# The last batch of an attention loop gets an order of its own: its two routers and a layernorm change places

## The reference

```python
x = _layernorm(x + _L0_attn_ref(x, Wq, Wk, Wv, Wo))      # 16 heads in 4 groups, head size 16
...
def _L0_attn_ref(x, Wq, Wk, Wv, Wo):
    ...
    scores = jnp.einsum('bqgrd,bkgd->bgrqk', q, k) * scale + bias     # causal, sqrt-distance bias
    attn = jax.nn.softmax(scores, axis=-1)
    o = jnp.einsum('bgrqk,bkgd->bqgrd', attn, v).reshape(B, S, Hd)
    return o @ Wo.T
...
# router: sigmoid scores over 32 experts, 4 of 8 groups of experts kept, 6 experts per token
w, idx = _gate(xf, gate_w)
c = jnp.zeros((T, E), xf.dtype).at[jnp.arange(T)[:, None], idx].add(w)
y = jnp.einsum('tei,te,edi->td', jax.nn.silu(g) * u, c, w22)          # g, u: xf by w11, w33 of each expert
shared = jax.nn.silu(xf @ sw1.T) * (xf @ sw3.T) @ sw2.T
...
x = _layernorm(x + y + shared)
```

## Time and profile before

| | |
|---|---|
| median of 3 runs | 549.81 us (547.13 to 551.17) |
| the profiled execution, its own time | 553.8 us |
| its span, first to last instruction | 552.0 us |
| mean granted clock of PE | 0.942 of full speed |
| busy PE, DVE, ACT, POOL | 467.1, 366.9, 321.2, 227.0 us |
| attention loop, body of batch 7 on DVE | 222.6 to 243.3 us of the span |
| stretch between the loops | 243.3 to 296.4 us |
| expert loop and the end | 296.4 to 552.0 us |

### The profile page before, as it was taken

The page is one execution under the profiler, slowest core; times in us unless marked ns, Lnnn a source line. Parts: engine busy times, 40 slices in busy tenths (PEclk is TensorE's granted clock), DMA queues, the critical chain, the costliest instruction groups (busy, mean ns, idle before and its releaser), DMA issues.

```text
span 552.0 us, 12954 instructions
## 1 busy us (share of the span) xinstructions
PE 467.1 (85%) x3218; PEld 387.1 (70%) x3219; DVE 366.9 (66%) x1711; ACT 321.2 (58%) x1087; POOL 227.0 (41%) x244
## 2 busy tenths in 40 slices
PE   4376778777988887879895999999999999999993
PEld 3254557665857565654354999999999999998772
DVE  4036477839596969887733776777777777771574
ACT  1069798848787888954102565555555555553024
POOL 0000000260616262747770656666666666664000
PEclk9769999869788879999997999999999999999998
DMA  4669659997768672339994555555555555521994
GB/s 134 147 227 263 145 138 269 248 258 191 195 156 209 165 197 60 132 107 409 417 415 123 161 166 157 154 157 164 152 159 150 171 162 164 156 73 59 420 416 172
DMA packets 67995, 107.91 MB, mean 196 GB/s; under 512 B 9189, under 2 KB 55018, under 8 KB 66416
## 3 DMA queue, kind: packets, MB, share of 16 engines
q1 hardware_dynamic: 53472, 74.62, 47.2%
q0 software_dynamic: 10752, 26.13, 14.3%
q10 hardware_dynamic: 3728, 6.65, 3.3%
HBM read 64.03 MB, written 43.33 MB: 195 GB/s over the span
## 4 chain that ended last, share of the span: by engine, by line
PE 45%; DMA 20%; DVE 9%; SPq 8%; POOL 6%; ACT 6%; issue 5%; POOLq 0%; ACTq 0%; DVEq 0%
PE bank L726 21%; PE bank L735 11%; POOL routed L1433 6%; DMA expert_w<-expert_out 6%; DMA k_scratch<-k_lo 5%; PE bank L716 5%; DMA k_pack<-k_scratch 4%; DVE s_neg L1012 4%; ACT probs L831 4%; SPq L431 3%; PE bank L500 3%; DMA xt<-xT 2%; SPq L382 1%; ACT pT L842 1%; SPq L396 1%
## 5 line engine op out<-in xcount | busy, mean ns | idle before, releaser
L1433 POOL DMA_INDIRECT routed<-rows,position x96 | 93.5, 974 | 193.3 <-DVE position L1176 164.9
L1443 POOL DMA_INDIRECT expert_out<-rows,out_row x128 | 130.8, 1022 | 84.7 <-issue 61.2
L831 ACT ACTIVATE probs<-s_neg,m_neg 128x128 f32<-128x128 f32 (+1 forms) x256 | 114.1, 450 | 43.6 <-DVE m_neg L1012 43.4
L1012 DVE CUSTOM_DVE_ANT_0 s_neg<-bank,bias_sb 128x128 f32<-128x128 f32 (+1 forms) x256 | 79.6, 352 | 59.6 <-PE bank L532 58.5
L930 ACT ACTIVATE eg<-bank 128x128 f32<-128x128 f32 x128 | 35.5, 278 | 83.5 <-PE bank L726 82.8
L735 PE MATMUL bank<-expert_w,ea 128*128 x256 | 78.4, 388 | 2.4 <-issue 0.9
L726 PEld LDWEIGHTS bank<-x1T,xn 128*128 128x128 f32 x512 | 67.8, 194 | 3.6 <-issue 0.3
L532 PE MATMUL bank<-k_pack,q_pack 128*128 128x256 f32 (+1 forms) x128 | 58.7, 467 | 13.5 <-DMA k_pack<-k_scratch 11.2
L726 PE MATMUL bank<-x1T,xn 128*128 128x128 f32 x512 | 68.5, 277 | 0.0
L937 ACT ACTIVATE rows<-bank,pick 128x256 f32<-128x256 f32 x128 | 60.1, 470 | 2.7 <-DVE out_row L1342 2.2
L920 ACT ACTIVATE x1T<-bank 128x256 f32<-128x256 f32 x128 | 49.3, 385 | 12.6 <-PE bank L716 12.6
(11 more groups left out here) (162 smaller groups left out, 807.0 us busy)
## 6 DMA issues: line engine op xcount, KB each, us to landing
xg_all<-routed SPq DMA_DIRECT2D x128, 137.5 KB, 2.2
expert_w<-expert_out SPq DMA_DIRECT2D x16, 768.0 KB, 13.0
expert_w<-expert_weights SPq DMA_DIRECT2D x9, 1024.0 KB, 17.8
q_pack<-q_scratch SPq DMA_DIRECT2D x32, 256.0 KB, 4.7
routed<-empty SPq DMA_DIRECT2D x8, 550.0 KB, 13.3
k_pack<-k_scratch SPq DMA_DIRECT2D x16, 256.0 KB, 6.9
expert_w<-expert_weights ACTq DMA_DIRECT2D x3, 1024.0 KB
xt<-xT SPq DMA_DIRECT2D x9, 256.0 KB, 7.1
```

The lines of the kernel that those rows point to most:

```text
L831: act.activation(probs[g % 2][qb][:, 2 * pair + r, :], s_neg[u][:, r, 0:n], ACT.Exp, bias=m_neg[:, u, r:r + 1], scale=-1.0, accum_out=row_ ...
L1012: dve.tensor_tensor_reduce(out=s_neg[u][:, r, 0:n], in0=SCORES[u][:, n * r:n * r + n], in1=bias_sb[:, REP * g + 2 * pair + r, SEQ - n:SEQ] ...
L1433: pool.indirect_dma_start(routed, bass.IndirectOffsetOnAxis(ap=position[b % ROW_BUFS][:, t, j:j + 1], axis=0), rows[b % ROW_BUFS][:, t, :] ...
L1443: pool.indirect_dma_start(expert_out, bass.IndirectOffsetOnAxis(ap=out_row[:, k:k + 1], axis=0), ey[k], None, bounds_check=TOKENS * TOPK - ...
```

## The change

Only the body of batch 7 (`ahead` is false) and what follows it are reordered; the instructions stay the same.

- The router of batch 5 is finished in groups 0 and 1 (`LAST_AT_UNIT`: piece 11 at unit (1, 3) in place of (3, 2)).
- Batch 6's layernorm moves up in the body: `project_out` to (1, 1), `ln_stats` to (1, 2), `ln_moments` and the root to (1, 3), `ln_apply` to (2, 0), `turn_x1` to (2, 1), `copy_x1t` to (2, 2), `gate` to (2, 3), that is ahead of `values(7, 0)` on PE; `gate_exps(6)` to the start of group 3.
- The router of batch 6 stands in group 3 on DVE (`LAST_NEXT_AT_UNIT`), all of it ahead of `invert(7, par, 1)`; its `ranks` stands at the end of PE's body, ahead of `values(7, 1)`.
- Behind the loop, batch 6's router is gone; `turn_x1(7)` stands between the two `shared_up(0, m)`, and ACT's `copy_x1t(7)` between the two `shared_silu(0, m)`.

```diff
# PE, body
-                        if g == 3 and u == 0 and two_behind:
+                        if (g, u) == ((3, 0) if ahead else (1, 2)) and two_behind:
                             ranks(b - 2, par)
-                        if g == 3 and u == 1 and one_behind:
+                        if (g, u) == ((3, 1) if ahead else (2, 1)) and one_behind:
                             turn_x1(b - 1, o)
+                        if (g, u) == (1, 1) and not ahead:
+                            project_out(b - 1, o)
+                        if (g, u) == (2, 3) and not ahead:
+                            gate(b - 1, o)
                     if g == 2:
                         values(b, par, 0)
...
+                if not ahead:
+                    ranks(b - 1, o)
# PE, behind the loop
             shared_up(0, 0)
+            turn_x1(last_b, 1)
             shared_up(0, 1)
-            ranks(last_b - 1, 0)
-            turn_x1(last_b, 1)
             gate(last_b, 1)
# ACT, body
+                    if g == 3 and not ahead:
+                        gate_exps(b - 1)
...
-                        if g == 2 and u == 2 and one_behind:
+                        if (g, u) == ((2, 2) if ahead else (1, 3)) and one_behind:
                             ln_first_root(b - 1)
-                        if g == 3 and u == 1 and one_behind:
+                        if (g, u) == ((3, 1) if ahead else (2, 2)) and one_behind:
                             copy_x1t(b - 1, o, h - 1 + par)
# ACT, behind the loop
-            gate_exps(last_b - 1)
             ln_first_root(last_b)
             shared_silu(0, 0)
+            copy_x1t(last_b, 1, last_b // 2)
             shared_silu(0, 1)
-            copy_x1t(last_b, 1, last_b // 2)
# DVE, body
+            LAST_AT_UNIT = {(0, 1): (0, 1), (0, 2): (2, 3), (0, 3): (4, 5), (1, 0): (6, 7), (1, 1): (8, 9), (1, 3): (10, 11)}
+            LAST_NEXT_AT_UNIT = {(3, 1): (0, 1, 2, 3, 4, 5), (3, 2): (6, 7, 8, 9), (3, 3): (10, 11)}
...
-                        if (g, u) == (2, 1) and one_behind:
+                        if (g, u) == ((2, 1) if ahead else (1, 2)) and one_behind:
                             ln_stats(b - 1, o, h - 1 + par)
-                        if (g, u) == (2, 2) and one_behind:
+                        if (g, u) == ((2, 2) if ahead else (1, 3)) and one_behind:
                             ln_moments(b - 1)
-                        if (g, u) == (2, 3) and one_behind:
+                        if (g, u) == ((2, 3) if ahead else (2, 0)) and one_behind:
                             ln_apply(b - 1, o, h - 1 + par)
                         if two_behind:
-                            for piece in AT_UNIT.get((g, u), ()):
+                            for piece in (AT_UNIT if ahead else LAST_AT_UNIT).get((g, u), ()):
                                 router_piece(b - 2, par, piece)
+                        if not ahead:
+                            for piece in LAST_NEXT_AT_UNIT.get((g, u), ()):
+                                router_piece(b - 1, o, piece)
# DVE, behind the loop
-            router_piece(b - 1, 0, 0)
             norm(b, 1, 1)
-            for piece in range(1, 6):
-                router_piece(b - 1, 0, piece)
             ln_stats(b, 1, b // 2)
             ln_moments(b)
-            for piece in range(6, 10):
-                router_piece(b - 1, 0, piece)
             ln_apply(b, 1, b // 2)
-            for piece in (10, 11):
-                router_piece(b - 1, 0, piece)
```

More of the change, by code:

```diff
@@ L632, in body @@
                         values(b - 1, o, 1)
-                    if g == 1 and one_behind:
+                    if g == 1 and one_behind and ahead:
                         project_out(b - 1, o)
-                    if g == 3 and one_behind:
+                    if g == 3 and one_behind and ahead:
                         gate(b - 1, o)
+                if not ahead:
+                    ranks(b - 1, o)
             pe.wait_ge(w_loaded, 16 * 3)
```

## The result

The changed kernel took 558.55 us (median of 4 runs, 553.0 to 560.86) beside 550.03 for the kernel before on the same chip: ratio 1.0154 [1.0102, 1.0205], some 8.5 us slower. The forecast had +3.5, and 558.5 as the upper end of its range. The profiled execution took 560.86 us with a span of 559.0 and a mean granted clock of 0.932.

What follows compares the result with a forecast made beforehand. Three chains ending within 4 us (POOL, DMA drain, shared expert) bound the kernel. N 10.3 us later moves the gate exps 11.1; less 6.5 slack and the cold first slot, the shared expert ends +3.5: 549.8 to 553.3 us, range 548 to 558.5.

Steps and rivals of the forecast that it cites:

- N: Moment the last norm of batch 7 raises `normed`, when the expert weights can start; forecast at 256.2, 10.3 us later.
- Groups 0 and 1: DVE's first two groups in body 7: with the added pieces they last 14.6 us, ending 3.6 us later.
- the give-back of `shared_up(0, 1)`: Behind N on PE, `shared_up(0, 1)` (3.67 us) before `gate` mostly cancels x1's earlier arrival; gate exps at N + 14.1.
- the wait of 9 us ahead of dispatch 7: POOL waits 9 us for batch 7's position; dispatch 7 starts at 278.6 in place of 275.16, +3.4.
- faster: Rival: N stays within 1.6 us, POOL's dispatches 5 to 7 run gapless, time falls by 5.4 to 544.4; chance 0.08.
- even: Rival: ACT's extra 1.6, the clock's 0.7 and a us in groups 0 and 1 are not paid; 550; chance 0.17.
- Not last, if the rows are not held by it.: DMA drain behind N: 16.5 MB, ending at 298.3, taken as not last unless it holds the rows.
- a sign against itself: Behind POOL's dispatches: the forecast falls if the scatters land long behind POOL's last issue; no size given.
- the DMA drain is last: Rival: weight packets hold the scatters, last landing at 300.7, second slot at 305.5, +5.7, 555.5 us; chance 0.17.
- The shared expert: Chain behind the loop: last add moves from 289.83 to 300.9, second slot at 303.3, +3.5 us, the last end.
- the clock at 0.7 us, looked for in group 3 alone: PE at 1.2 GHz for `values(7, 1)` after idling 246.9 to 252: 0.7 us on N, bounds 0 and 2.5.
- PE comes to them at full clock: First expert slots: full clock saves the first slot's 1.0 us, so POOL's chain delays the second slot +2.4.

Runs made afterwards that it cites:

- e11: Changed kernel plus 23 unread matmuls filling PE's holes in body 7, three of them ahead of `gate`; ratio to the kernel before 1.0106 [1.0048, 1.0165].
- e2: Changed kernel with batch 6's router back behind the last norm and PE's and ACT's old tail order; 549.03 us, ratio to the kernel before 1.0056.
- e4: Kernel before with 22 waiting copies on DVE ahead of the last norm of batch 7; ratio 1.0121 [1.0086, 1.0156].
- e12: Kernel before with ACT's 3 MB of expert weights issued only after all scatters have landed; 551.76 us, ratio 1.0077.
- e8: Kernel before with SP's nine weight loads held until ACT has copied batch 7's x1, some 10 us later; 552.38 us, ratio 1.0100.
- the repeat: The changed kernel measured once more, nothing altered; 554.97 us beside 546.41 for the kernel before, ratio 1.0163 [1.0131, 1.0195].
- e7: Changed kernel plus 20 unread matmuls on PE in the last batch, none at unit (2, 3); ratio to the kernel before 1.0097 [1.0062, 1.0133].
- e14: Changed kernel with PE's and ACT's order behind the loop as in the kernel before; ratio to the kernel before 1.0123 [1.0085, 1.016].
- e1: Changed kernel plus 38 unread matmuls in PE's holes of the last batch, 16 at unit (3, 2); ratio to the kernel before 1.0202 [1.015, 1.0255].
- e3: Kernel before with only batch 5's router finished early, in groups 0 and 1 of the last body; 546.73 us, ratio 1.0007.
- e9: Kernel before with ACT's 3 MB of expert weights issued behind its last shared silu; 549.48 us, ratio 1.0045.

## Why the prediction was wrong

**The order was priced rightly.** At full clock (e11) dispatch 5, dispatch 6, N, the exps and dispatch 7 came within 0.9 us of the forecast's moments. N came to 0.1, with some luck: its sum held 0.7 for a low clock that e11 doesn't have, and the router's end was 0.5 late. Groups 0 and 1, the 6.1 us of pieces ahead of `position`, the give-back of `shared_up(0, 1)`, the wait of 9 us ahead of dispatch 7 (10.5 after, 7.9 in e11) are right. The rivals *faster* and *even* are refuted by N, 13 to 15 us later in the two profiles after.

**The step that failed: "Not last, if the rows are not held by it."** The drain itself was forecast at T + 76.7, N + 42.1; it came at 76.2 in e11, and at N + 41.7 there as in the first profile after. But the sum let the rows land 3.8 us behind POOL's last issue, at 75.8, and they are held: they landed at 77.8, 1.6 us behind the drain. The prediction had named this as a sign against itself. The landing of before, 2.4 us behind the drain of its own, was the same thing and was read as a property of POOL's last issue. In the eleven profiles in which weights are still moving at POOL's last issue and well behind it, the landing lies 0 to 2.4 us behind the drain, however far behind the last issue's start (4.4 to 11.2 us). In e2 and e4 the last scatter's own data are the last on the queues, and it lands 2.9 to 3.0 us behind its issue; in e12, with no weights beside it, 2.5. e8 shows the holding with nothing else moved. So N, which sets when SP's weights start, had none of the slack that the forecast gave it: the rival *the DMA drain is last* is the mechanism. Its 555.5 is near what the kernel takes when the clock holds (1.0106 times 549.81 is 555.6, the interval 552.4 to 558.9), in part by luck: the landing came 1.3 us ahead of the rival's, and what followed took as much more. The shared expert, which the forecast put last, ended 0.9 us ahead of the landing in e11; in the first profile it ended 0.7 and in the repeat 0.9 us behind it, and PE still waited for the rows. Of the 2.3 us by which e11's third slot comes behind the forecast, 0.7 is the first slot's later start; the rest is the first two slots, 1.84 and 1.82 us, mostly at the low clock after 3.8 us of waiting for the rows.

The Trainium skill's page "DMA: Bandwidth & Descriptors" (Queues, rings and completion order) states besides the taking of turns that the increment of a DMA's semaphore is written only after every earlier write of that DMA engine, across its queues. e8 (11.24 us from issue to landing) and e12 (2.50) agree with both. No run here tells the two apart, so whether the data or only the semaphore comes late stays open.

**The second step that failed: the clock at 0.7 us, looked for in group 3 alone.** The sum had PE idle "between about 246.9 and 252" and nowhere else. The clock fell earlier first, in short waits for a DVE that now carries batch 5's router, and stayed low through group 2, where the whole chain turn, gate, values, transposes lies on the path: 8.5 us from `turn_x1` to the copy of the sums, against 6.1 in e11 and 5.8 forecast. In group 3 pieces 10 and 11 covered only part of it (DVE waits 1.44 us for the second sums). In the profiles it costs 3.0 us of N and 3.1 of the third slot (repeat against e11), 5.0 in the first one after, so in the repeat it is the larger part of the 5.4 us by which the third slot misses the forecast. The times don't show it: 1.0163 and 1.0106 have overlapping intervals, e11 carries 23 extra matmuls, and e7, whose profile has N at 38.6, measured 1.0097. So the clock's share of the 8.5 us, some 3, rests on single profiles.

At the fall in group 2, or at most 1.3 us ahead of it, lies a wait of PE: 1.34 us after and in the repeat, e2 and e14, 1.75 us in e7. The Trainium skill's page "TensorE: Matmul & The Clock Gate" (A second HAM failure mode) tells of another kernel in which frequent short idle times between groups of matmuls made the clock go back and forth between its two levels; the falls here are like it. But a wait of that length is not enough. In the kernel before, PE waited as long ahead of `turn_x1`, and the clock was 1.00 through that stretch:

```profile
240.44 0.66 PE L546 MATMUL bank<-cst,probs 128*128 128x128 f32 x4 [1.46 <-ACT probs L831]
```

```profile
238.00:246.00 8.00, 5.40 (x68) 4.21 (x64) 6.50 (x27) 4.63 (x16) 2.33 (x3) 1.00 0.26 89
```

In e8 it stood idle for 2.50 us ahead of 269.66, and the clock was 1.00 from 266 to 272. What else has to come together for a fall stays open; with the holes filled, in e1 and e11, it did not come in body 7.

**Smaller.** "PE comes to them at full clock" holds after for the first slot (1.18 us) and not for the next (1.91): the clock fell at 305.5, behind a wait of 2.23 us for the rows. From N to the exps the forecast had 14.1 us; e11 took 13.4, the repeat 15.1, with the old order of the tail (e14) 14.6, so that order hardly matters.

**Why the change loses.** It moves 6 us of router ahead of N so that dispatch 5 can start 4 to 5.5 us and dispatch 6 0.6 to 4.7 us earlier; but the rows wait for the weights, the weights start at N, and the last dispatch waits for a gate that hangs on N as well. e2, which gives N 6.6 us of this back, takes back 5.9 of the repeat's 8.6 us; e3, in which N moves by 2.2 us and more scatters go out ahead of it, loses and wins nothing. None of the versions beat the kernel before.

## What to carry to other kernels

Where small scatters share the DMA engines with bulk loads that end later, take the landing from the end of the bulk traffic and not from the last issue, and ask of each edit when it lets the bulk start. A gap on a busy queue is worth closing only if what waits behind its last item moves too: list the positions of all later items first. And look for PE's new holes in every group whose supplier becomes later, not only in the longest one; then price the whole dependent chain behind the hole at the low level.

## What was not expected of the hardware

An f32 matmul with 256 columns stands in the trace as two instructions, 0.46 us in all (2.76 us for 6). In e8 the DMA engines ran full, at 399 to 427 GB/s in stretches of 1 and 2 us, for 7.5 us behind the end of POOL's last issue, with its scatters not yet landed. And 3 MB of weights issued late held back a load of rows (8.04 us in e12, where it took 2.08) more than they held the last scatter (6.51 us in e9, where it takes 2.50 with no weights beside it).
